# A two-layer AdaLN block on one core: the layer-0 scan's outputs over four banks, its gates on GpSimd, its constant term between the residuals

## The reference

```python
mod = (_silu(L0_c) @ L0_wmod).reshape(L0_c.shape[0], 6, 1, -1)
sa, ca, ga, sb, cb, gb = (mod[:, 0], mod[:, 1], mod[:, 2], mod[:, 3], mod[:, 4], mod[:, 5])
ga = (2 * (ga >= 0) - 1) * jnp.maximum(jnp.abs(ga), 0.25)
h = _layernorm(x, axis=-1) * (1 + ca) + sa
# _L0_attn_ref(h, ...):
delta = sigmoid(einsum('bsd,od->bso', h, W_t) + b_t) * 0.99 + 0.01
Bu = einsum('bsd,nd->bsn', h, W_b) + b_b
A_exp = exp(A[None, None, :] * delta)
_, s = associative_scan(_scan_combine, (A_exp, Bu), axis=1)
y = einsum('bsn,dn->bsd', s, W_c) + b_c + h * D[None, None, :]
y = einsum('bsd,od->bso', y, W_o) + b_o
x = x + ga * y
h = _layernorm(x, axis=-1) * (1 + cb) + sb      # feeds the layer-0 experts
```

## Time and profile before

| | |
|---|---|
| device time, median of 3 runs | 961.08 us |
| span of the profiled execution | 1008.9 us |
| busy: TensorE, VectorE, ScalarE, GpSimd | 838.6, 592.7, 371.3, 255.6 us |
| mean granted TensorE clock | 0.890 |
| end of the copy of the last logits (line 824) | 101.24 us |

### The profile page before, as it was taken

The page is one execution under the profiler, slowest core; times in us unless marked ns, Lnnn a source line. Parts: engine busy times, 40 slices in busy tenths (PEclk is TensorE's granted clock), DMA queues, the critical chain, the costliest instruction groups (busy, mean ns, idle before and its releaser), DMA issues.

```text
span 1008.9 us, 22593 instructions
## 1 busy us (share of the span) xinstructions
PE 838.6 (83%) x8710; PEld 572.5 (57%) x8710; DVE 592.7 (59%) x1638; ACT 371.3 (37%) x719; POOL 255.6 (25%) x252
## 2 busy tenths in 40 slices
PE   5545698999958789999999999986679789999960
PEld 3443365656634446656656656553257578888850
DVE  8632866666688787687687687763245232222217
ACT  3335221222214105435435436553325324444424
POOL 0522000000073601012011112034661514444440
PEclk9956699999989958999999999997688779999985
DMA  5600022226414761133233332121310417777746
GB/s 147 268 3 0 1 92 92 92 92 211 140 49 140 233 174 48 29 95 89 46 94 60 74 94 62 31 59 34 86 41 9 131 55 213 212 220 215 212 130 223
DMA packets 107827, 108.37 MB, mean 107 GB/s; under 512 B 48892, under 2 KB 93644, under 8 KB 106796
## 3 DMA queue, kind: packets, MB, share of 16 engines
q1 hardware_dynamic: 103196, 97.82, 33.7%
q0 software_dynamic: 4544, 9.35, 2.6%
HBM read 82.15 MB, written 44.78 MB: 126 GB/s over the span
## 4 chain that ended last, share of the span: by engine, by line
PE 62%; DVE 18%; issue 7%; ACT 5%; POOL 3%; DMA 3%; SPq 2%; POOLq 0%; DVEq 0%; ACTq 0%
PE bank L2148 8%; PE bank L2158 7%; PE bank L1928 7%; PE bank L1762 5%; PE bank L1773 5%; PE bank L1774 4%; PE bank L1868 4%; DVE sb_arena L1360 4%; PE bank L2077 3%; PE bank L1820 3%; PE bank L2067 3%; PE bank L1846 3%; DVE sb_ST L1023 2%; DVE sb_arena L1350 2%; DVE sb_arena L1352 2%
## 5 line engine op out<-in xcount | busy, mean ns | idle before, releaser
L1360 DVE TRANSPOSE_TENSOR_REDUCE sb_arena<-bank 128x16 f32<-128x512 f32 x192 | 120.3, 685 | 25.4 <-PE bank L1868 24.2
L901 ACT ACTIVATE sb_arena<-bank 128x512 f32<-128x512 f32 x192 | 99.2, 602 | 50.0 <-PE bank L1868 50.0
L989 ACT ACTIVATE sb_arena<-bank,sb_arena 128x256 f32<-128x256 f32 x156 | 65.3, 471 | 99.9 <-PE bank L2148 99.1
L749 POOL DMA_INDIRECT expert_results<-sb_arena x78 | 74.7, 958 | 105.5 <-DVE sb_arena L1619 88.9
L1762 PEld LDWEIGHTS bank<-sb_arena 128*128 128x128 f32 x512 | 67.9, 195 | 42.1 <-issue 25.3
L858 ACT ACTIVATE sb_arena<-bank 128x512 f32<-128x512 f32 x64 | 38.2, 597 | 143.9 <-PE bank L1774 143.8
L2148 PE MATMUL bank<-sb_arena 128*128 128x256 f32 x312 | 80.3, 402 | 3.8 <-DVE sb_arena L1615 1.8
L1928 PE MATMUL bank<-sb_arena 128*16 128x128 f32 x1024 | 71.9, 422 | 9.5 <-issue 9.4
L1762 PE MATMUL bank<-sb_arena 128*128 128x128 f32 x512 | 70.2, 281 | 10.5 <-DVE sb_arena L1192 10.5
L741 POOL DMA_INDIRECT dispatched_rows<-sb_arena x64 | 63.0, 984 | 62.7 <-DVE sb_arena L1525 44.4
L2158 PE MATMUL bank<-sb_arena 128*128 128x128 f32 x624 | 75.9, 275 | 0.0
(11 more groups left out here) (263 smaller groups left out, 1356.5 us busy)
## 6 DMA issues: line engine op xcount, KB each, us to landing
sb_arena<-in_w SPq DMA_DIRECT2D x39, 578.0 KB
dispatched_rows<-in_padding SPq DMA_DIRECT2D x8, 2064.0 KB, 9.5
sb_arena<-dispatched_rows SPq DMA_DIRECT2D x39, 129.0 KB
sb_arena<-q_parts SPq DMA_DIRECT2D x8, 512.0 KB, 5.5
sb_arena<-k_parts SPq DMA_DIRECT2D x8, 512.0 KB, 7.0
context_rel<-sb_arena SPq DMA_DIRECT2D x256, 8.0 KB
sb_arena<-expert_results SPq DMA_DIRECT2D x16, 256.0 KB, 5.9
q_parts<-sb_arena SPq DMA_DIRECT2D x24, 128.0 KB, 2.4
```

Of the source, the lines that this page charges most:

```text
L749: nc.gpsimd.indirect_dma_start(yD[:, :], bass.IndirectOffsetOnAxis(ap=rid[:, k, r:r + 1], axis=0), YS[:, k, r, :], None).then_inc(s_yo[k], 16)
L901: nc.scalar.activation(dst, src, ACT.Exp).then_inc(s_ex, 1)
L1360: v.tensor_reduce(dst.rearrange("p h b -> p (h b)"), bank[r % RING][:, :].rearrange("p (b c) -> p b c", c=32), AX, ALU.max, apply_transpos ...
```

## The change

TensorE: `outputs(c)` writes bank 4 + c % 4 and waits for the gating of chunk c-4 where it waited for that of c-2; the second transposes of c-4 stand behind the outputs of c, where those of c-3 stood. The gate matmuls come ahead of the transposes of chunk 1. ScalarE copies gates, `CW` (the 128x128 product) and output bias (`BO`) out of PSUM, normalises chunks 5 and 7 of the first normalisation (`normalise1st` now serves both), and in the second takes the deviation of c+1, normalises c and scales the transposes of c-1. The sigmoid becomes 0.5 + 0.5 tanh(z/2), its constants folded into the exponent's scale and bias. GpSimd computes the gates, `M2` and `ZM`, and adds the constant term to chunks 0 and 1, then to c+2 after the residual of c. VectorE loses this work, and the modulation copies move ahead by one chunk.

```diff
@@ -645,22 +647,50 @@
             nc.gpsimd.memset(ones[:, :], 1.0).then_inc(s_set, 1)
-            pool.wait_ge(s_vb, 16)
-            pool.wait_ge(s_xn, NC)
-            for c in range(NC):
+            pool_chain = [0]
+            def in_turn(ins):
+                pool_chain[0] += 1
+                ins.then_inc(s_pl, 1)
+                pool.wait_ge(s_pl, pool_chain[0])
+            pool.wait_ge(s_const, 16 * 2)
+            nc.gpsimd.tensor_scalar(M2[:, :], WoT[:, :], raw[:, 3:4], None, ALU.mult)
+            G4, twice = GG[:, 0:4, :], GT1[:, :, :]
+            pool.wait_ge(s_gev, 1)
+            in_turn(nc.gpsimd.tensor_scalar(G4, twice, 0.0, 0.5, ALU.is_ge, ALU.subtract))
+            in_turn(nc.gpsimd.tensor_tensor(twice, twice, G4, ALU.mult))
+            in_turn(nc.gpsimd.tensor_scalar(twice, twice, 0.25, 2.0, ALU.max, ALU.mult))
+            nc.gpsimd.tensor_tensor(G4, G4, twice, ALU.mult)
+            pool.wait_ge(s_gev, 2)
+            in_turn(nc.gpsimd.tensor_tensor(BO[:, :], BO[:, :], borow[0:B, :], ALU.add))
+            nc.gpsimd.tensor_tensor(GG[:, 4, :], BO[:, :], GG[:, 0, :], ALU.mult).then_inc(s_gg, 1)
+            for b in range(8):
+                ins = nc.gpsimd.tensor_scalar(ZM[:, b, :], CW[:, :], blockmask[:, b:b + 1], None, ALU.mult)
+            ins.then_inc(s_zm, 1)
+            def constant_term(c):
+                pool.wait_ge(s_xn, c + 1)
...
                                         ).then_inc(s_x0, 1)
-            pool.wait_ge(s_x0, NC)
...
                 pool.wait_ge(s_gt, u + 1)
+                pool.wait_ge(s_x0, c + 1)
...
+            pool.wait_ge(s_vb, 16)
+            for c in range(2):
+                constant_term(c)
...
                 residual(c, c)
+                if c + 2 < NC:
+                    constant_term(c + 2)
@@ -792,57 +822,64 @@
-            for c in range(6):
+            def steps0(h):
+                act.wait_ge(s_ssm, h + 1)
+                nc.scalar.activation(EZ[:, h, :], bank[2 + h][:, S:2 * S], ACT.Tanh, scale=0.5,
+                                     bias=small[:, 0:1]).then_inc(s_ez, 1)
+                act.wait_ge(s_ez, h + 1)
+                nc.scalar.activation(AE[:, h, :], EZ[:, h, :], ACT.Exp, scale=small[:, 1:2],
+                                     bias=small[:, 2:3]).then_inc(s_ae, 1)
+            def normalise1st(n, c):
+                act.wait_ge(s_nbm, 2 + c + 1 if n else 1 + c // 7)
+                wait(act, s_tr, n * NC + c - 1)
+                for T in range(c * TPC, (c + 1) * TPC):
+                    if T % TPC == TPC - 1 and n == 0:
+                        act.wait_ge(s_xn, c)
+                    ins = nc.scalar.activation(XN[:, c % 2, T % TPC, :], X[:, T, :], ACT.Identity,
+                                               scale=RSTD[:, T:T + 1], bias=NB[:, T:T + 1])
+                ins.then_inc(s_xn, 1)
+            for c in range(4):
...
             features0(0, 0)
+            deviation(0, 4)
+            act.wait_ge(s_mod, 2)
+            nc.scalar.activation(GT1[:, :, :].rearrange("p g f -> p (g f)"), bank[1][0:B, :], ACT.Copy, scale=2.0
+                                 ).then_inc(s_gev, 1)
             features0(0, 1)
+            act.wait_ge(s_m1, 1)
+            nc.scalar.copy(CW[:, :], bank[4][:, 0:D])
+            nc.scalar.copy(BO[:, :], bank[5][0:B, 0:D]).then_inc(s_gev, 1)
+            deviation(0, 5)
+            features0(0, 2)
             deviation(0, 6)
-            features0(0, 2)
+            features0(0, 3)
             deviation(0, 7)
-            def steps0(h):
-                act.wait_ge(s_ssm, h + 1)
-                nc.scalar.activation(EZ[:, h, :], bank[2 + h][:, S:2 * S], ACT.Exp, scale=-1.0,
-                                     bias=small[:, 0:1]).then_inc(s_ez, 1)
-            def decays0(h):
-                act.wait_ge(s_sig, h + 1)
-                nc.scalar.activation(AE[:, h, :], SIG[:, h, :], ACT.Exp, scale=small[:, 1:2],
-                                     bias=small[:, 2:3]).then_inc(s_ae, 1)
-            for c in range(3, 6):
-                features0(0, c)
+            normalise1st(0, 5)
+            features0(0, 4)
+            features0(0, 5)
+            normalise1st(0, 7)
...
             features0(0, 7)
-            decays0(0)
             steps0(1)
-            decays0(1)
...
-            def normalise1st(c):
-                act.wait_ge(s_nbm, c + 1)
-                wait(act, s_tr, NC + c - 1)
-                for T in range(c * TPC, (c + 1) * TPC):
-                    ins = nc.scalar.activation(XN[:, c % 2, T % TPC, :], X[:, T, :], ACT.Identity,
-                                               scale=RSTD[:, T:T + 1], bias=NB[:, T:T + 1])
-                ins.then_inc(s_xn, 1)
+            deviation(1, 0)
             for c in range(NC):
-                deviation(1, c)
-                if c >= 2:
-                    normalise1st(c - 2)
-                if c >= 3:
-                    features0(1, c - 3)
-            normalise1st(6)
-            features0(1, 5)
-            logits_out(0)
-            normalise1st(7)
-            features0(1, 6)
-            features0(1, 7)
+                if c + 1 < NC:
+                    deviation(1, c + 1)
+                normalise1st(1, c)
+                if c:
+                    features0(1, c - 1)
+                if c == 5:
+                    logits_out(0)
+            features0(1, NC - 1)
@@ -1034,14 +1071,16 @@
                 wait(dve, s_tr, n * NC + c - 1)
+                if c == 6:
+                    dve.wait_ge(s_xn, c)
...
-            def scales0(c):
-                dve.wait_ge(s_sd, NC + c + 1)
+            def scales0(n, c):
+                dve.wait_ge(s_sd, n * NC + c + 1)
@@ -1056,46 +1095,27 @@
                 dve.wait_ge(s_const, 16 * 2)
-                v.tensor_scalar(small[:, 0:1], raw[:, 2:3], -1.0, None, ALU.mult)
-                v.tensor_scalar(small[:, 1:2], raw[:, 1:2], 0.99, None, ALU.mult)
-                v.tensor_scalar(small[:, 2:3], raw[:, 1:2], 0.01, None, ALU.mult)
+                v.tensor_scalar(small[:, 0:1], raw[:, 2:3], 0.5, None, ALU.mult)
+                v.tensor_scalar(small[:, 1:2], raw[:, 1:2], 0.495, None, ALU.mult)
+                v.tensor_scalar(small[:, 2:3], raw[:, 1:2], 0.505, None, ALU.mult)
...
             first_statistics(3)
+            modulations()
...
             first_statistics(4)
-            modulations()
...
             first_statistics(5)
+            scales0(0, 5)
...
             first_statistics(7)
-            for c in range(5, NC):
-                normalise0(0, c)
-            dve.wait_ge(s_mod, 2)
-            dve.wait_ge(s_m1, 1)
...
-            v.tensor_scalar(M2[:, :], WoT[:, :], raw[:, 3:4], None, ALU.mult)
-            for b in range(8):
-                ins = v.tensor_scalar(ZM[:, b, :], bank[4][:, 0:D], blockmask[:, b:b + 1], None, ALU.mult)
-            ins.then_inc(s_zm, 1)
+            scales0(0, 7)
+            normalise0(0, 6)
@@ -1132,21 +1152,20 @@
                 dve.wait_ge(s_ez, h + 1)
-                link(v.tensor_scalar(SIG[:, h, :], EZ[:, h, :], 1.0, None, ALU.add))
-                v.reciprocal(SIG[:, h, :], SIG[:, h, :]).then_inc(s_sig, 1)
...
                 v.tensor_tensor_scan(HSC[:, h, :], AE[:, h, :], BU[:, h, :], 0.0, ALU.mult, ALU.add).then_inc(s_hs, 1)
+            v.tensor_copy(identb[:, :].rearrange("p (a k) -> p a k", a=4), ident[:, :].rearrange("p (k a) -> p a k", a=4))
...
                     dve.wait_ge(s_y, c + 1)
-                    gated(c, bank[4 + c % 2][:, :].rearrange("p (b t f) -> p b t f", b=2, t=2), 0, 0)
+                    gated(c, bank[4 + c % 4][:, :].rearrange("p (b t f) -> p b t f", b=2, t=2), 0, 0)
...
                 if c >= 2:
-                    scales0(c - 2)
+                    scales0(1, c - 2)
@@ -1672,12 +1691,12 @@
             transposes0(0, 0)
-            transposes0(0, 1)
...
             ins.then_inc(s_mod, 1)
+            transposes0(0, 1)
@@ -1706,11 +1725,11 @@
                 pe.wait_ge(s_hs, c // 4 + 1)
-                wait(pe, s_gt, c - 1)
+                wait(pe, s_gt, c - 3)
...
                     b = T // 2
-                    dst = bank[4 + c % 2][:, t * D:(t + 1) * D]
+                    dst = bank[4 + c % 4][:, t * D:(t + 1) * D]
@@ -1738,13 +1757,15 @@
                 outputs(c)
-                if c >= 3:
-                    transposes0(1, c - 3)
-            transposes0(1, 5)
+                if c >= 4:
+                    transposes0(1, c - 4)
+            transposes0(1, 4)
...
             logits0(0)
+            transposes0(1, 5)
+            pe.wait_ge(s_gt, NC)
+            logits_back(0)
             transposes0(1, 6)
-            logits_back(0)
```

More of the change, by code:

```diff
@@ L98, in build @@
         GT1 = sb("GT1", [B, 4, D])
+        BO = sb("BO", [B, D])
         ST = sb("ST", [P, NT, 6])
@@ L142, in build @@
         ZM = R.take(8 * D).rearrange("p (b o) -> p b o", b=8)
+        CW = R.take(D)
         EZ = R.take(2 * S).rearrange("p (h t) -> p h t", h=2)
```

(6 more changed lines are left out.)

12 lines of the change are left out of this document (removed).

## The result

The changed kernel took 931.44 us (median of 4 runs, 926.74 to 933.65), the kernel before 961.65 (956.97 to 963.09, 4 runs). The ratio is 0.9691 (95% interval 0.9653 to 0.9729): 30.2 us less, where 931 was forecast.

The account below looks back on a forecast made before the run. No engine was taken as the limit: engines took turns at 48 to 89 us, after late constant terms. Stage savings of 31.8 us, discounted to 30 for TensorE's clock, gave 961.1 - 30 = 931, range 923 to 944.

Parts of the forecast that it names:

- The turn: Second normalisation, 48 to 89 us: engines take turns, 8.43 us per chunk, because PE's and ScalarE's orders tie chunks together.
- The pace: Second normalisation after the change: ScalarE should be the slowest engine and set 2.65 us per chunk.
- Before the outputs: First normalisation to second scan: longest chain on ScalarE, second scan ending near 37.9 against 40.08, first outputs at 36.0.
- The outputs: Outputs through last logits copy: first gating at 38.0, ScalarE 2.65 per chunk, copy at 69.4 against 101.24, saving 31.8 us.
- The gates: Gate arithmetic on GpSimd: gates at 23.7 us, or 26.2, against 30.6, with 5.5 us of cover before gating.
- the mixed chunks: Three chunks in the outputs stretch that, with TensorE at its low clock, would cost 4.5 us each in place of 2.65.
- rival 1: TensorE sets the pace at half clock for more chunks: 4 to 7 us of gain lost, 935 to 938; chance 0.22.
- The discount of 1.8 us: Allowance for TensorE running at the low clock, lowering the expected saving from 31.8 to 30 us.
- The sum: Stage savings of 31.8 us, reduced to 30 for TensorE's clock and carried over whole: 961.1 - 30 = 931.
- Rival 2: GpSimd becomes the late engine through gates, scalings and constant terms: saving 23 us, time 938; chance 0.11.
- rival 3: Some order still ties chunk to chunk, 4.2 us per chunk over two chunks: saving 19, time 942; chance 0.06.
- rival 4: Slower: later part loses the gain through TensorE's clock, 5% of 581.5 us being 29; chance 0.06 together with no change.

Follow-up runs that it names:

- the control: The changed kernel run again without edit, in the third group of runs, against the kernel before: 981.09 us against 1016.89, ratio 0.9671.

## Why the prediction was right, and where its steps were not

*The turn.* Right, and shown. The order on ScalarE and TensorE made the 8.43 us turn, not the banks: order alone gives 24.5 us, banks alone 0.5. The prediction credited the gain to the change as a whole; the two experiments split it. The constants give 5.1 by themselves. 24.5 and 5.1 come to 29.6, and the whole change reaches 28.6, so the parts beside them (banks, early gates, tanh) seem to add nothing to those two, though tanh is worth 1.5 within the whole. That is a sum of two single effects; order and constants together, with the rest as before, were not run. Part of what is missing is seen: from the first statistics to the copy the order alone takes 28.3 us, the whole change 29.75, and 0.8 of that difference is small scales that the constants between residuals lengthen.

*The pace.* Forecast 2.65 per chunk, by ScalarE; measured 2.63, and extra work on ScalarE came out at the end (2.1 us for seven pairs of copies). This is mechanism, not luck.

*Before the outputs.* This step was mis-sized. The second scan was to end near 37.9, before the 40.08 of the kernel before; it ends at 40.39. The first outputs were to start at 36.0 and start at 38.35, later than the 36.63 before. So the new work before the outputs saved nothing there; the stage starts earlier only because the constants no longer stand ahead of it. Two rows of VectorE's timeline before (L1039 normalising, L1047 a small scale):

```profile
16.67 1.11 DVE L1039 TENSOR_SCALAR sb_XN<-sb_X,sb_MV,sb_RSTD 128x128 f32<-128x128 f32 x4
...
51.83 0.16 DVE L1047 SCALAR_TENSOR_TENSOR sb_NB<-sb_MV,sb_RSTD 128x4 f32<-128x4 f32 x1
```

VectorE's timeline after (L1086 scales, L1078 normalising, L1157 scan, L1060 statistics):

```profile
16.58 1.48 DVE L1078 TENSOR_SCALAR sb_XN<-sb_X,sb_MV,sb_RSTD 128x128 f32<-128x128 f32 x4
...
19.83 0.84 DVE L1086 SCALAR_TENSOR_TENSOR sb_NB<-sb_MV,sb_RSTD 128x4 f32<-128x4 f32 x1
...
20.80 1.39 DVE L1078 TENSOR_SCALAR sb_XN<-sb_X,sb_MV,sb_RSTD 128x128 f32<-128x128 f32 x4
...
23.48 1.89 DVE L1078 TENSOR_SCALAR sb_XN<-sb_X,sb_MV,sb_RSTD 128x128 f32<-128x128 f32 x4
...
39.70 0.69 DVE L1157 TENSOR_TENSOR_SCAN sb_arena<-sb_arena 128x256 f32<-128x256 f32 x1 [0.21 <-ACT sb_arena L830]
...
42.90 0.86 DVE L1060 BATCH_NORM_STATS2 sb_ST<-sb_X 128x6 f32<-128x128 f32 x4
...
46.50 1.05 DVE L1086 SCALAR_TENSOR_TENSOR sb_NB<-sb_MV,sb_RSTD 128x4 f32<-128x4 f32 x1
...
49.51 0.50 DVE L1086 SCALAR_TENSOR_TENSOR sb_NB<-sb_MV,sb_RSTD 128x4 f32<-128x4 f32 x1
```

A chunk (four normalisations of 128x128) took 1.11 before; three chunks take 1.48, 1.39 and 1.89 here beside GpSimd's gates, and a small scale of 0.16 takes 0.84. I charged what the two engines lose beside each other to GpSimd's chain, "under 1 us", and to VectorE nothing; added up, VectorE lost 0.37 + 0.28 + 0.78 + 0.68 = 2.1 us on the path to the last statistics of the first normalisation, which end at 26.57 where I had 24.4. The run with the gates on VectorE shows it: there every chunk takes 1.11 and the scale 0.16, and the second scan starts 1.6 us earlier (it ends only 0.7 earlier, since it has the constants beside it).

*The outputs.* "In the outputs VectorE's large operations have one SBUF input, so neither changes the sum": true of the large ones. The small scales have two. At 46.50 one takes 1.05 and ends at 47.55; GpSimd's residual beside it started at 46.27 and took 1.27, until 47.54. The next ends at 50.01, GpSimd's at 49.99. The Trainium skill (SBUF — State Buffer, Who interferes with whom) calls the ports that VectorE shares with GpSimd an exclusive lock, and says that a VectorE instruction with two SBUF inputs contends with a GpSimd instruction that reads SBUF. These rows agree, and the run with one input in PSUM shows it: 0.16 everywhere, 0.80 us gained. The prediction weighed the rule only as VectorE holding up GpSimd, and put it aside for the outputs. What the rows show is VectorE held up by GpSimd, and it was worth 0.8 us there.

*The gates.* Forecast 23.7 (26.2 at worst), measured 24.97. The two-step tensor_scalar of 16x512 takes 1.94, outside the rows' bounds of 0.73 to 1.26, between them and the doubled cost (2.52) that I named; the scalings take 0.6 each (4.76 for eight), not 0.4. Neither mattered: the gate tile's transfer is issued at 27.06 and takes 7.0 us, and gating starts at 40.51.

*TensorE's clock.* TensorE's timeline (L1722 second projections, L1734 first outputs, L1684 transposes):

```profile
36.49 1.93 PE L1722 MATMUL bank<-sb_arena 128*32 128x256 f32 x32 [2.76 <-ACT sb_arena L820]
38.35 0.49 PE L1734 MATMUL bank<-sb_arena 128*128 128x128 f32 x2
...
49.29 0.66 PE L1684 MATMUL bank<-sb_ident,sb_XN 128*128 128x128 f32 x4 [1.74 <-ACT sb_XN L839]
...
57.01 0.66 PE L1684 MATMUL bank<-sb_ident,sb_XN 128*128 128x128 f32 x4 [0.19 <-ACT sb_XN L839]
59.64 1.11 PE L1684 MATMUL bank<-sb_ident,sb_XN 128*128 128x128 f32 x4 [1.97 <-ACT sb_XN L839]
```

The granted clock is 1.00 from 44 to 58 us and 0.66 from 58 to 73. The transposes between outputs run at the high level (0.66 for four) until 57.01; once the outputs are done and TensorE idles between them, the last four groups take 1.11, 0.76, 0.66 and 1.12. So the mixed chunks were not at the low level, and rival 1 did not happen in this trace. The discount of 1.8 us that I made for it was used up by something else, the time that VectorE lost beside GpSimd.

*The sum.* The copy was worked out at 69.4 and ends at 72.65, 3.25 late. The first gating was to start at 38.0 and starts at 40.51, 2.5 late, of which 2.1 are VectorE's loss. Normalising chunk 0 was to start at 44.2 and starts at 47.59, 3.4 late: 0.9 more, the first small scale of 1.05. From there to the end of the copy it is 25.1, and 25.2 was the sum. Saved by the stages 28.6 against 31.8, and 30 forecast after the discount. That 931 was met to 0.4 us is luck: a discount for one thing covered another, and the kernels' runs lie 6 to 7 us apart.

*The rivals and the signs.* Rival 2 (GpSimd late) is refuted by GpSimd's own idle 7.2 us ahead of 41.35 and by the constants in a block; rival 3 by 2.63 per chunk; rival 4 by the ratio, and by the control's in another group. One sign of being wrong that I named did appear: "if later stages differ in length by more than 3 us". The stretch behind the first dispatch took 100.5 us in place of 151.9. The control, with the same kernel, took 147.9 there, so it is not the change's doing; but as I had put it, the sign could not tell the two apart.

## What to carry to other kernels

When a chain of waits shows the same few instructions of four engines in turn, each for one chunk, look in the written orders for the instruction that stands behind a wait of a later chunk; more buffers alone do nothing while it stands there. Where work is moved to GpSimd, list what VectorE does beside it, small instructions with two SBUF inputs included, and charge both engines. Two remedies for one wait (early gates, interleaved constants) need not add up: try each alone. And a gain of 5 us in a stage can be read from the stage and not from a total whose runs lie 14 us apart.

## What the runs showed of the hardware that was not expected

- A VectorE instruction of 128x4 with two SBUF inputs took up to 1.05 us beside a GpSimd instruction of 1.27, against 0.16 alone and 0.16 with one input in PSUM.
- Instructions with one SBUF tensor input lose time beside GpSimd too: four 128x128 tensor_scalar took 1.39 to 1.89 us against 1.11, and in the run with the gates on VectorE a cast of 128x128 took 1.27 against 0.25.
- On GpSimd a tensor_scalar with two operations took 1.94 us for 16x512, more than a two-input multiplication (1.25).
- TensorE's level in the second projections differed between executions of nearly the same front: 1.93 us in the first profile after and the control, 3.53 with the constants in a block, where the second scan starts 1.5 us later than in the first profile after. What decides it was not tried.
- The stretch from the dispatch to the first expert results took 100.5 us in one execution and 144 to 156 in all others profiled, with the same code.
